# Moving jobs, table loads and counts inside the selective-scan part of a fused block, one core

## The reference

```python
x = x + mamba(keep_top_rows(x, cond))          # rows of smaller norm are set to zero first
x = x + ffn(attention(x, cond, mask))          # attention with one query per head, then an MLP

# mamba, per batch, 512 inner channels, 16 states:
xi, z = split(rmsnorm(x) @ in_proj)
xi = silu(causal_conv(xi) + conv_b)            # 4 taps
dt, Bm, Cm = split(xi @ x_proj)
delta = softplus(dt @ dt_w + dt_b)
h_t = exp(delta_t * A) * h_(t-1) + (delta_t * xi_t) * B_t
y_t = sum over states of h_t * C_t, plus xi_t * D
x + (y * silu(z)) @ out_proj
```

## Time and profile before

| | |
|---|---|
| median of 3 runs (range) | 535.56 us (535.3 to 538.06) |
| the profiled execution | 537.52 us |
| its span, first to last instruction | 535.7 us |
| busy: PE, DVE | 447.7 us (84%), 448.6 us (84%) |
| busy: ACT, POOL | 382.0 us (71%), 382.0 us (71%) |
| steps (scans), chunks 0, 1, 2, 3 begin | 42.82, 160.37, 269.94, 377.10 us |
| mean granted TensorE clock | 0.950 of full speed |

### The profile page before, as it was taken

How to read it: one execution, slowest core, us unless ns; L and a number is a source line. 1 busy time by engine, 2 the same in 40 slices (tenths; PEclk the granted TensorE clock), 3 DMA queues, 4 the chain that set the end, 5 groups by cost and what they waited for, 6 DMA issues and landing times.

```text
span 535.7 us, 8150 instructions
## 1 busy us (share of the span) xinstructions
PE 447.7 (84%) x2865; PEld 333.6 (62%) x2865; DVE 448.6 (84%) x527; ACT 382.0 (71%) x673; POOL 382.0 (71%) x235
## 2 busy tenths in 40 slices
PE   7957898769767988898879988977799877989991
PEld 5443765457547655665766656645798766877650
DVE  4778899977999899889998998899997999882143
ACT  4685787678987797879877988798666888751210
POOL 5139968866999589868997699679977999820001
PEclk9997899977999999999999999999897899899996
DMA  8531111110012111100111111011111187009204
GB/s 277 158 122 40 40 40 40 39 44 11 29 39 89 62 47 40 43 6 34 42 40 40 43 53 59 9 40 40 40 40 40 40 294 306 1 26 345 92 1 162
DMA packets 18422, 39.58 MB, mean 74 GB/s; under 512 B 1943, under 2 KB 10775, under 8 KB 18376
## 3 DMA queue, kind: packets, MB, share of 16 engines
q1 hardware_dynamic: 18376, 39.00, 21.0%
HBM read 36.76 MB, written 2.23 MB: 73 GB/s over the span
## 4 chain that ended last, share of the span: by engine, by line
PE 35%; DVE 34%; issue 16%; ACT 13%; DMA 1%; DVEq 0%; SPq 0%; ACTq 0%
DVE scanmem L1944 22%; PE hT L968 7%; DVE yTd L1955 7%; PE pp L593 5%; PE pp L692 4%; ACT dA L1440 3%; PE yacc L662 3%; PE pp L653 2%; PE dA L930 2%; ACT hc L1450 2%; DVE yTd L1870 1%; PE pp L760 1%; PE pp L902 1%; PE pp L623 1%; PE yacc L658 1%
## 5 line engine op out<-in xcount | busy, mean ns | idle before, releaser
L1598 POOL TENSOR_TENSOR scanmem<-par,scanmem 128x1024 f32<-128x1024 f32 x128 | 300.1, 2367 | 67.9 <-PE hT L968 46.0
L968 PE MATMUL hT<-con,scanmem 128*128 128x128 f32 x1008 | 162.1, 291 | 53.8 <-DVE yTd L1955 39.2
L1440 ACT ACTIVATE dA<-par,Aneg 128x512 f32<-128x512 f32 x256 | 172.1, 690 | 42.6 <-DVE scanmem L1944 40.9
L968 PEld LDWEIGHTS hT<-con,scanmem 128*128 128x128 f32 x1008 | 120.3, 148 | 102.3 <-DVE yTd L1955 34.7
L1944 DVE TENSOR_TENSOR_SCAN scanmem<-dA,carry,scanmem 128x512 f32<-128x512 f32 x128 | 156.4, 1264 | 10.6 <-ACT dA L1440 9.4
L1944 DVE TENSOR_TENSOR_SCAN scanmem<-dA,scanmem 128x512 f32<-128x512 f32 x128 | 148.8, 1204 | 10.5 <-ACT dA L1440 8.9
L1450 ACT ACTIVATE hc<-hT,CTs 128x512 f32<-128x512 f32 x127 | 86.1, 678 | 27.6 <-PE hT L968 26.4
L662 PE MATMUL yacc<-con,hc 128*128 128x128 f32 x512 | 82.7, 287 | 0.0
L1955 DVE SCALAR_TENSOR_TENSOR yTd<-hT,CTs,yTd 128x512 f32<-128x512 f32 x90 | 65.3, 725 | 7.0 <-PE hT L968 5.8
L662 PEld LDWEIGHTS yacc<-con,hc 128*128 128x128 f32 x512 | 65.2, 150 | 0.2
L593 PE MATMUL pp<-xnT,wi 128*128 128x512 f32 x120 | 58.6, 616 | 4.2 <-ACT xnT L1193 2.5
(11 more groups left out here) (227 smaller groups left out, 510.5 us busy)
## 6 DMA issues: line engine op xcount, KB each, us to landing
scanmem<-brow SPq DMA_DIRECT2D x32, 512.0 KB, 3.6
par<-in SPq DMA_DIRECT2D x1, 4096.0 KB, 17.9
scanmem<-in SPq DMA_DIRECT2D x1, 4096.0 KB, 14.5
xt<-in SPq DMA_DIRECT2D x4, 512.0 KB, 6.9
wi<-in SPq DMA_DIRECT2D x2, 1024.0 KB, 7.4
out<-par SPq DMA_DIRECT2D x3, 512.0 KB, 3.9
aw<-in SPq DMA_DIRECT2D x5, 256.0 KB, 7.6
xr<-in SPq DMA_DIRECT2D x1, 1024.0 KB, 9.6
```

The costliest lines, as they stand in the source:

```text
L968: last = nc.tensor.transpose(hT[:, i % 2, m * P:(m + 1) * P], hb[:, n % RING, m, i * P:(i + 1) * P], ident)
L1440: A(dA[:, m % 2, :], delta(c)[:, m, :], ACT.Exp, scale=Aneg[:, m * NS + s:m * NS + s + 1]).then_inc(da_ready, 1)
L1598: nc.gpsimd.tensor_tensor(hb[:, n % RING, ms, :], dx(c)[:, ms, :], Bb[:, row:row + 1, :].to_broadcast([P, 2, T]), ALU.mult).then_inc(bx_re ...
```

## The change

- The table loads leave `after_job`. The load of the table with Ln (LN_TABLE_AT = 8) now comes in step 8 of chunks 0 to 2, between exponentials 1 and 2; the load back (TANH_TABLE_AT = 12) in step 12 at the same place.
- O of chunks 0 and 1 is four jobs of one block each, at h = 15, 17, 18 and 23, where it was two jobs of two blocks at h = 18 and 20. LAST_EPILOGUE (O of chunk 2) stays as it was.
- Chunk 1's preparation (which runs in chunk 0) gets its own places: XT at h = 17, D 0 and D 1 at 18 and 19, D 2 and D 3 stay at 21 and 22. Ahead of that XT, PE runs eight matmuls of the identity whose result nobody reads (WARM_XT).
- The counts of batch 1 are in steps 0 to 5, 8 and 10, and POOL ends the ranking at step (1, 0) in place of (0, 13).
- Head: XT of chunk 0 goes to bank 1 of `dA` and no longer waits for D's reading; ACT waits for the reading of D 2 before it reads XT. Z 0 and Z 1 run on PE at the end of the head, behind XT, and are read at h = 0; Z 2 and Z 3 both run at h = 0.

```diff
-EPILOGUE = {1: [("Y", 1), ("Y", 3)], 18: [("O", 0)], 20: [("O", 1)], 28: [("R", 0)], 30: [("R", 1)]}
+FIRST_STEPS = {17: [("XT", 0)], 18: [("D", 0)], 19: [("D", 1)], 20: [], 21: [("D", 2)], 22: [("D", 3)]}
+EPILOGUE = {1: [("Y", 1), ("Y", 3)], 15: [("O", 0)], 17: [("O", 2)], 18: [("O", 1)], 23: [("O", 3)], 28: [("R", 0)], 30: [("R", 1)]}
...
-KEPT_AT = GB + 5
+COUNT_AT = (0, 1, 2, 3, 4, 5, 8, 10)
+KEPT_AT = NS
+LN_TABLE_AT, TANH_TABLE_AT = 8, 12
...
-    return slots(PROLOGUE, n)
+    return slots(PROLOGUE if n > 1 else {**PROLOGUE, **FIRST_STEPS}, n)
...
+FIRST_Z = [("Z", 0, 0), ("Z", 0, 1)]
...
-    head += [("X", 0, 0)] + [("D", 0, m) for m in range(CT)] + [("XT", 0, 0)]
+    head += [("X", 0, 0)] + [("D", 0, m) for m in range(CT)] + [("XT", 0, 0)] + FIRST_Z
...
-            for m in range(CT):
-                beside[m // 2] += [("Z", 0, m)]
+            beside[0] += [("Z", 0, m) for m in range(2, CT)]
...
-    return BESIDE[h - 1] if h else []
+    return BESIDE[h - 1] if h else FIRST_Z
...
+WARM_XT = 8
...
+            if n == 0 and name == "XT":
+                return dA[:, 1, :]
...
+                if n == 1:
+                    keep_warm(WARM_XT, o[:, 0:P])
                 wait_read(pe, ("X", n, 0))
...
-                for i in range(1 if e == NCH - 1 else 2):
+                for i in range(2 if e == NCH - 2 else 1):
...
+                elif n == 0 and name == "XT":
+                    wait_read(pe, ("I", 0, 3))
+                elif job in FIRST_Z:
+                    wait_read(pe, ("D", 0, 1 - m))
...
             run(("XT", 0, 0))
+            for job in FIRST_Z:
+                run(job)
...
-                if name == "X" and n:
-                    exp_ln_table()
                 if name == "D":
                     softplus(n, i)
-                    if n and i == CT - 1:
-                        act.preload_act_table_set("exp_and_others")
...
+            wait_read(act, ("D", 0, 2))
             read(("XT", 0, 0))
...
+                if n == 0 and m == 1:
+                    wait_read(act, ("XT", 0, 0))
...
+                    if c + 1 < NCH and s == LN_TABLE_AT:
+                        exp_ln_table()
+                    if c + 1 < NCH and s == TANH_TABLE_AT:
+                        act.preload_act_table_set("exp_and_others")
                     exp_step(n, 2)
...
-                        wait_full(pool, ("O", n - 2, 1))
+                        wait_full(pool, ("O", n - 2, NT - 1))
...
-                if s < GB:
+                if s in COUNT_AT:
+                    i = COUNT_AT.index(s)
                     own.after()
-                    last = count(GB + s, magrow, junk)
-                    if s < GB - 1:
+                    last = count(GB + i, magrow, junk)
+                    if i < GB - 1:
```

More of the change, by code:

```diff
@@ L733, in job_R @@
                 wait_read(pe, ("O", e, j))
-                if e == NCH - 1:
+                if e != NCH - 2:
                     wait_read(pe, ("O", e, j + 2))
```

## The result

The changed kernel takes 531.58 us (median of 4 runs, 530.8 to 533.11) where the kernel before took 536.81 in the same comparison (4 runs, 535.3 to 539.99). The ratio is 0.9868, with a 95% interval of [0.9829, 0.9907]: 7.1 us less by the ratio (5.0 to 9.2), 5.2 by the two medians. The forecast was 12.6 less and 523.0, in a range of 517.6 to 529.7. So the change is faster, as was foretold, but the time lies above the range. The profiled execution took 533.11, with a span of 531.3.

What follows compares the result with a forecast made beforehand. DVE's work bounds the kernel, so only its idle time can be won, mostly scans waiting for exponentials. Chunks 0, 1, 2 and head, 5.1 + 3.0 + 3.2 + 1.3 = 12.6 us, give 523.0 from 535.56; range 517.6 to 529.7.

Steps and rivals of the forecast that it cites:

- the table loads: Steps 8 and 12 of chunks 0 to 2: moved loads win 3.5 us plus 0.8 at each load back.
- O in four jobs: Chunks 1 and 2: four smaller O jobs remove waits for PE, 2.4 us beside the table loads.
- gaps before step 9 below 0.6: Sign of being right: gaps before the first scan of step 9 below 0.6 in chunks 0 to 2.
- no second O's wait: Sign of being right: no wait like the second O's 2.58 on ACT in step 10.
- POOL should not take it back: Change of chunk: POOL's input of step (1, 0) has 8.2 us to spare; the ranking takes 1.3 of that.
- the mark of the starts: Sign of being right: scans begin at about 154 in chunk 1, 260.5 in chunk 2, 364.5 in chunk 3.
- POOL becomes the bound: Rival, chance 0.04: POOL sets the pace at two changes of chunk, some 10 of 12.6 given back: 533.
- the head's 1.3: First steps of chunk 0: earlier Z and XT close gaps, 1.3 us less, bounds −0.5 to +2.6.
- chunk 0's 5.1: Chunk 0's stages with the loads, D and XT: idle 1.59 + 5.30, less 1.8 left, gives 5.1 us.
- Clock 1.00 in chunk 0's stage of D: Sign of being right: PE's granted clock there is 1.00; it was 0.50 over 114 to 127.
- Only the table loads pay: Rival, chance 0.18: O and D still hold up the turning, the head gives nothing; 5.9 us less, 529.7.
- The forecast's last rival but one: Slower, chance 0.03: PE at half clock in steps 7 to 11, 0.31 us lost for each us; 543.

Runs made afterwards that it cites:

- e1_tables: Kernel before with only the two table loads moved; 533.36 us, ratio 0.9872.
- e4_kept13: Changed kernel with the end of the ranking back in step (0, 13); 528.17 us, ratio 0.9795.
- e6_kept13_no_head: Changed kernel with the ranking back in step (0, 13) and without the head's part; 528.38 us, ratio 0.9832.
- e11_hold_sum13_dve: e9_kept13_hold with the last block of step (0, 13) multiplied and added by DVE, not ACT and POOL; 525.43 us, ratio 0.9748.
- e3_head: Kernel before with the head part alone; 539.17 us, ratio 1.0007.
- e9_kept13_hold: Changed kernel with the ranking back in step (0, 13) and eight unread products in step (0, 1); 526.11 us, ratio 0.9776.
- e2_o_split: Kernel before with only O of chunks 0 and 1 in four jobs; 536.63 us, ratio 0.9958.
- e15_hold_twice: e12_hold_no_warm_xt with eight unread products also in each of steps (0, 15) and (1, 0); 524.68 us, ratio 0.9728.
- e16_hold_no_first: e9_kept13_hold with D and XT of chunk 1 in their old places, without the eight products ahead of XT; 523.83 us, ratio 0.9733.
- e12_hold_no_warm_xt: e9_kept13_hold without the eight unread products ahead of XT of chunk 1; 522.94 us, ratio 0.9706.
- e8_kept_late: Kernel before with only the end of the ranking moved from step (0, 13) to (1, 0); 543.53 us, ratio 1.0101.
- e5_no_head: Changed kernel without the head's part; 530.07 us, ratio 0.9846.
- e14_hold_late: Changed kernel with eight unread products in step (0, 1), ranking still at (1, 0); 526.59 us, ratio 0.9761.
- e10_kept13_no_first: e4_kept13 with D and XT of chunk 1 in their old places, without the eight unread products; 527.63 us, ratio 0.9797.
- e13_hold_no_head: e6_kept13_no_head with eight unread products in step (0, 1); 528.32 us, ratio 0.9796.

## Why the prediction was wrong, and where it was right

**Right: the table loads.** Forecast 5.9 us, alone 6.9 (4.3 to 9.4), and the rows show the gaps around steps 9 and 12 as forecast: none before step (0, 9) and 0.25 in step (0, 12), and in chunks 1 and 2 at most 0.07 that waits for an exponential.

**Right: O in four jobs.** The wait of 2.58 is gone, alone 2.3 us (0.5 to 4.0). Both sums were careful on the safe side: I had left 1.6 and 1.9 us of idle time in steps 8 to 12 of chunks 1 and 2. The profile has 0.24 + 0.56 = 0.80 and 0.07 + 0.39 + 0.16 = 0.62, which is most of why these stages gave 8.6 and not 6.2. As marks, "gaps before step 9 below 0.6" and "no second O's wait" came true.

**Wrong: "POOL should not take it back".** The step that failed is the slack of 8.2 us, worked out from rows 9. These rows pair POOL's input of step (1, 0) with its scan, 10.6 us apart. POOL's queue is in order, and the next to be wanted was not that input but the addition of step (0, 13) that stood further on in the queue, with 0.44 to spare. The second half of the step failed too: "POOL follows the turning of four steps before, which comes earlier too". The turning of step (0, 10) came 0.65 earlier, since PE did it at half clock (13.7 us of it, from 119.9 to 133.6, the same length as in the kernel before). In e1_tables the input behind that turning began at 131.36, 2.48 earlier than before, the ranking was done long ahead of it, and the change of chunk cost nothing. The mark set for this, a wait of the scans for POOL's input, did not come as it was written: it is a mac that waits, for the addition. But the mark of the starts shows the step: chunk 1 should have begun at about 154 and began at 160.22, and chunks 2 and 3 began at 267.31 and 371.06 and not at 260.5 and 364.5. The 6.2 us that were missing at the start of chunk 1 are nearly all that was missing in the end.

What it cost is less plain than where it was. The stage at the change of chunk lost 4.01. With the ranking late it takes 30.03 to 30.06 in three profiles (29.27 without the head's part), all with 6.8 us at half clock. With the ranking back it takes 29.22 with as much half clock (e4_kept13) and 26.91 with none (e6_kept13_no_head). So some 0.8 of the 4.01 goes with the ranking, some 2.3 with the half clock, and 0.9 is left, with a wait for POOL of 0.76. e6_kept13_no_head has that wait and kept its clock, and e11_hold_sum13_dve has no wait and lost it: that the wait brings the half clock is not shown. The rival *POOL becomes the bound* had the right place, a chance of 0.04, and with 10 us given back too high a price.

**Wrong: the head's 1.3.** The bounds were −0.5 to +2.6 and the profile has −1.1 (−1.5 with the start); the runs with and without the part show no difference (e3_head 1.0007 [0.9975, 1.0039]). The forecast did see an idle PE and a falling clock, but it looked only at Z 2 and Z 3, right behind the idle time that it foresaw. The idle time that mattered came later, 3.01 us ahead of a turning, after Z 2 and Z 3 had gone from the queue. At full clock the three steps take 22.68 (e9_kept13_hold), which is 24.15 − 22.68 = 1.47 less than the old head in e2_o_split at nearly full clock, close to the 1.3 taken. That is with eight unread products which the forecast did not have. The Trainium skill (TensorE: Matmul & The Clock Gate, "HAM oscillation — how this bites in real kernels") tells of products that wait mid-run for their data (there, for a DMA) and then start again at half rate. The rows agree: 3.01 us of waiting, and 0.50 over 55.5 to 65.0. Whether holding the clock pays is another question: it did where nothing urgent was queued behind the unread products (e9_kept13_hold, in the profile), and did not where the reduction was (e15_hold_twice).

**Wrong in its reason: chunk 0's 5.1.** The stage gave 4.18, which looks near. But its largest part, some 2.6 of the 5.1 beside the two table loads, was to come of D and XT early, and no run shows a gain of it (1.4 us, within the intervals, between e16_hold_no_first and e12_hold_no_warm_xt). 2.2 us of the idle time was the clock of one execution: e3_head has the same code there and does not show it. "Clock 1.00 in chunk 0's stage of D" failed as well, and D's additions wait there (lines of after):
```profile
117.08 0.69 DVE L1763 SCALAR_TENSOR_TENSOR par<-pp,par 128x512 f32<-128x512 f32 x1 [1.48 <-ACT par L1305]
133.14 0.69 DVE L1763 SCALAR_TENSOR_TENSOR par<-pp,par 128x512 f32<-128x512 f32 x1 [1.01 <-ACT par L1305]
```
The 1.48 was forecast as 0.9. The eight products took 1.95 us at full clock (109.0 to 110.9), where the estimate had 1.4.

**The sum.** 523.0 was 0.9766 of the 535.56 on which it was made. The changed kernel with its ranking in place and its clock held in the head has 0.9776 (e9_kept13_hold). That the two agree is in part luck: the loads and O gave more than their terms, D's place and the head nothing that can be measured. It is luck as well that the changed kernel (0.9868) stands where the rival *Only the table loads pay* would have it (529.7, 0.989) and where e1_tables is (0.9872): O in four jobs pays by itself, and the costs took as much back. Two costs of the change were missed: 0.9868 − 0.9776 is 0.0092, 4.9 us.

**The clock's share.** The record has the mean granted clock of every execution, and the profiles have two levels of it, 1.00 and 0.50. So the time at half clock of an execution can be estimated as 2 × (1 − mean clock) × span; it is 32 to 72 us. Between executions of one kernel, each us of it goes with 0.23 us of time (0.20 to 0.26; 164 executions, correlation 0.79). The forecast's last rival but one had 0.31. With this slope all kernels can be set to the same time at half clock, again an estimate:

| kernel | at half clock, us | below the kernel before, us, at equal time at half clock |
|---|---|---|
| the kernel before | 54.5 | 0 |
| the changed kernel | 65.5 | 9.5 ± 1.3 |
| e4_kept13, ranking back | 59.7 | 11.9 ± 1.1 |
| e9_kept13_hold, and the clock held | 49.1 | 12.0 ± 1.1 |
| e12_hold_no_warm_xt | 39.6 | 12.4 ± 1.1 |
| e1_tables | 50.3 | 5.3 ± 1.1 |
| e2_o_split | 59.6 | 3.3 ± 0.8 |
| e3_head | 54.0 | −0.4 ± 0.8 |
| e8_kept_late | 62.3 | −3.0 ± 1.1 |

So the 5.5 us between forecast and result are some 2.5 of more time at half clock (11.0 × 0.23), some 2.4 of the ranking, and a small rest. The ranking late costs 2.4, 3.0, 2.8 and 1.3 us in the four pairs that differ in it alone (the changed kernel and e4_kept13; e8_kept_late and before; e5_no_head and e6_kept13_no_head; e14_hold_late and e9_kept13_hold), each ± 1.1 to 1.6. By the ratios as they are these were 3.9, 5.4, 0.8 and −0.8 us. What holding the clock brings (e9_kept13_hold against e4_kept13) is the clock itself and nothing beside it: 11.9 and 12.0. The eight products ahead of XT make no difference at equal time at half clock either (0.3 and 0.4 us, of opposite sign, in the two pairs without and with them).

**Open.** Whether D and XT early are worth anything: at equal time at half clock 2.0 ± 1.5 us by e10_kept13_no_first against e4_kept13, where the products come and go with them, and 0.1 ± 1.4 by e16_hold_no_first against e12_hold_no_warm_xt. Why the stretches at half clock fall where they do: in the 18 profiles they add up to 39 to 72 us, in other places in each, and the times of one kernel lie some 2 to 10 us apart. Whether the ranking, when it is late, brings more of them (the 2.4 to 3.0 above do not count that). And why it costs over 2 us at equal clock, where the wait that it adds for POOL is 0.96 in e8_kept_late.

## What to carry to other kernels

The slack of an in-order queue is the least over all the consumers of what is in it, so look for the pair of lines with the shortest way between the end of the one and the start of the other, not for the nearest to the edit; and see what the queue's first instruction waits for, as it won't come earlier only because its neighbours do. When work is taken out from beside a waiting TensorE, look for the longest idle time that is left after the edit, anywhere up to the next turning that another engine waits for. And a gap at half clock in one profile is not yet a cost of the code: see whether another execution with the same code there has it, before it is counted as something to win. Where every execution comes with its mean granted clock, compare kernels at equal time at half clock as well as by their medians.

## What the runs showed of the hardware

- Steps without a half clock repeat between kernels: (1, 3) to (1, 7) take 32.97 to 32.99 us in all 18 profiles.
- An execution is 0.23 us longer for each us in which the granted clock is 0.50 (164 executions, correlation 0.79), an estimate from their mean clocks.
- A stretch at half clock outlasts what led to it, but not always by as much: in the changed kernel 3.01 us of idle PE were followed by some 10 us at 0.50, and 3.50 us by 6.8; in e10_kept13_no_first 3.02 us at the same place went with 3.4.
- Eight unread 128x128 products (16 records, 1.95 us) in the idle place of step (0, 1) went with a clock of 1.00 from 55 to 65 us in e9_kept13_hold, and with steps (0, 0) to (0, 2) 3.5 us shorter than in e4_kept13. With the old head (e13_hold_no_head) the same products ran at half clock themselves, in 3.62 us.
- A table load of 1.28 us beside scans cost DVE nothing in step (0, 8), and the exponential behind it started 0.02 after the load's end: loaded at 104.76, next exponential at 106.06.
